# A decoder layer on one core: exponential before clip in the cross attention, key sums on TensorE

## What is computed

```
q, k, v = (x @ Wq.T + bq), (ctx @ Wk.T + bk), (ctx @ Wv.T + bv)     # per head
scores = einsum('bhsd,bhtd->bhst', q, k) / sqrt(32)
scores = clip(scores, -50, 50)
scores = where(attend, scores, -10000)
scores = clip(scores, -50, 50)
probs  = softmax(scores, axis=-1)
probs  = probs / (probs.sum(axis=-1, keepdims=True) + 1e-8)
ctx    = einsum('bhst,bhtd->bhsd', probs, v)
delta  = layernorm(rs * (ctx @ Wo.T + bo)) * gamma + beta
x      = layernorm(x + delta)
```

## Time and profile before

| | |
|---|---|
| median of three runs | 1547.76 us (1546.38 to 1550.83) |
| profiled execution | 1548.03 us |
| its span | 1546.1 us |
| mean granted clock of PE | 0.963 |
| PE, DVE, ACT, POOL busy in the span | 90%, 81%, 50%, 48% |
| DVE clip (line 1081), 64 instructions | 1213 ns each (median) |
| ACT exponential (line 1276), 64 instructions | 79.0 us, 1239 ns each |
| POOL sum of halves (line 1338), 32 instructions | 76.1 us, 2378 ns each |

### The profile page before, as it was taken

One profiled execution on the slowest core, in us unless ns is written; L12 is line 12 of the kernel. 1 busy time (PEld: TensorE's weight loads), 2 busy tenths in 40 slices (PEclk: granted clock), 3 DMA queues, 4 the chain that ended last, 5 costly groups with the idle time before them and its releaser, 6 DMA issues.

```text
span 1546.1 us, 25019 instructions
## 1 busy us (share of the span) xinstructions
PE 1395.2 (90%) x8338; PEld 1093.7 (71%) x8338; DVE 1257.5 (81%) x2029; ACT 766.7 (50%) x1710; POOL 744.2 (48%) x781
## 2 busy tenths in 40 slices
PE   5899999999999999999999999779999996359985
PEld 4788888888888888888888888667766674213332
DVE  6988888888888888888888888456899998759996
ACT  4444544444544445455455554444444444048885
POOL 4334334335235234334334333624766676547984
PEclk9999999999999999999999999989999998668998
DMA  5401101101011011012121110410000004004433
GB/s 206 163 2 42 64 6 41 50 19 41 27 42 41 27 42 28 22 49 68 42 69 55 34 61 15 143 42 15 15 15 14 14 1 170 0 20 91 90 87 95
DMA packets 73380, 79.91 MB, mean 52 GB/s; under 512 B 46007, under 2 KB 46519, under 8 KB 72893
## 3 DMA queue, kind: packets, MB, share of 16 engines
q1 hardware_dynamic: 73276, 78.73, 16.6%
HBM read 59.83 MB, written 8.40 MB: 44 GB/s over the span
## 4 chain that ended last, share of the span: by engine, by line
PE 40%; DVE 35%; issue 11%; POOL 11%; ACT 2%; DMA 1%; DVEq 1%; SPq 0%; POOLq 0%; ACTq 0%
PE psum L326 9%; PE psum L328 8%; PE psum L327 8%; DVE rope_b L513 6%; PE psum L367 3%; DVE p L522 3%; DVE total_e L526 3%; DVE xe L1081 2%; DVE acc L556 2%; DVE s L494 2%; DVE xinv L1088 2%; PE psum L388 2%; DVE rope_a L513 2%; PE psum L376 1%; PE psum L365 1%
## 5 line engine op out<-in xcount | busy, mean ns | idle before, releaser
L730 POOL TENSOR_TENSOR qk<-rope_a,rope_b 128x512 f32<-128x512 f32 x128 | 177.3, 1385 | 569.2 <-DVE rope_b L513 569.2
L326 PE MATMUL psum<-x_hi,w_hi 128*128 128x512 f32 x512 | 210.5, 411 | 11.2 <-POOL w_lo L724 11.2
L328 PE MATMUL psum<-x_hi,w_lo 128*128 128x512 f32 x512 | 201.2, 393 | 0.0
L327 PE MATMUL psum<-x_lo,w_hi 128*128 128x512 f32 x512 | 200.5, 392 | 0.0
L513 DVE SCALAR_TENSOR_TENSOR rope_b<-psum,qk_bias,sin 64x512 f32<-64x512 f32 x256 | 192.0, 750 | 3.7
L604 ACT ACTIVATE e<-s 128x384 f32<-128x384 f32 x128 | 66.4, 519 | 242.9 <-DVE s L494 242.9
L494 DVE SCALAR_TENSOR_TENSOR s<-psum,tri 128x384 f32<-128x384 f32 x128 | 70.7, 552 | 121.3 <-PE psum L367 121.3
L326 PE MATMUL psum<-w_hi,x_hi 128*128 128x256 f32 x512 | 147.4, 288 | 0.0
L327 PE MATMUL psum<-w_lo,x_hi 128*128 128x256 f32 x512 | 144.7, 283 | 0.0
L328 PE MATMUL psum<-w_hi,x_lo 128*128 128x256 f32 x512 | 144.6, 282 | 0.0
L1276 ACT ACTIVATE xe<-xe,mask_now 128x1024 f32<-128x1024 f32 x64 | 79.0, 1239 | 129.1 <-DVE xe L1081 129.1
(11 more groups left out here) (179 smaller groups left out, 3890.1 us busy)
## 6 DMA issues: line engine op xcount, KB each, us to landing
stage<-w_self_dram SPq DMA_DIRECT2D x64, 256.0 KB, 2.9
w_raw<-w_ffn_dram SPq DMA_DIRECT2D x32, 512.0 KB, 3.6
acc<-xT_dram SPq DMA_DIRECT2D x4, 1024.0 KB, 7.6
acc<-x_dram SPq DMA_DIRECT2D x1, 4096.0 KB, 15.1
w_signs<-w_sign SPq DMA_DIRECT2D x16, 256.0 KB, 2.1
c_raw<-ctxT_dram SPq DMA_DIRECT2D x8, 512.0 KB, 3.6
xstage<-w_cross_dram SPq DMA_DIRECT2D x16, 256.0 KB, 2.9
w<-w_signs SPq DMA_DIRECT2D x2, 2048.0 KB, 11.4
```

Source lines behind the costliest of these rows:

```text
L326: pe.matmul(ps, ah, bh, start=n == 0, stop=False)
L327: pe.matmul(ps, ah, bl, start=False, stop=False)
L328: last = pe.matmul(ps, al, bh, start=False, stop=n == len(pairs) - 1)
L730: nc.gpsimd.tensor_tensor(qk[:, k % 2, which, :], rope_a[:, which, :], rope_b[:, which, :], ALU.add).then_inc(qk_ready, 1)
```

## The change

Three things, all in `cross_attention`:

- `exps` reads the scores from the banks and writes `e`; it counts up `exped`, which also frees the banks for the next scores. It waits for the scores (`s_mm`) once per chunk.
- `clip` follows it, in place in SBUF, with exp(50) and exp(-50) as bounds, once per half, and waits for `exped` of its half. It counts up `e_ready`.
- `sum_e`, `e_sum` and its semaphore are gone. PE multiplies both halves of `e` with the ones, eight matmuls in place of four, and adds them in the bank.

```diff
@@ score
-                wait(pe, clipped, (b * CH + c) * HALVES)
+                wait(pe, exped, (b * CH + c) * HALVES)
@@ mix
-                pe.wait_ge(e_summed, b * CH + c + 1)
-                for h in range(HEADS_IN):
-                    last = pe.matmul(psA[h * H:(h + 1) * H, S:2 * S], ones[:], e_sum[:, h, :], start=True, stop=True,
-                                     tile_position=(0, h * H))
+                for kt in range(HALVES):
+                    for h in range(HEADS_IN):
+                        last = pe.matmul(psA[h * H:(h + 1) * H, S:2 * S], ones[:],
+                                         e[:, c % 2, h, kt * S:(kt + 1) * S], start=kt == 0, stop=kt == 1,
+                                         tile_position=(0, h * H))
@@ clip
-                dve.wait_ge(s_mm, b * CH + c + 1)
-
                 for kt in range(HALVES):
-                    nc.vector.tensor_scalar(e[:, c % 2, :, kt * S:(kt + 1) * S], scored[:, :, kt, :], LIMIT, -LIMIT,
-                                            ALU.min, ALU.max).then_inc(clipped, 1)
+                    dve.wait_ge(exped, (b * CH + c) * HALVES + (kt + 1))
+                    part = e[:, c % 2, :, kt * S:(kt + 1) * S]
+                    nc.vector.tensor_scalar(part, part, EXP_MOST, EXP_LEAST, ALU.min, ALU.max).then_inc(e_ready, 1)
@@ exps
-                act.wait_ge(clipped, (b * CH + c) * HALVES + (kt + 1))
-                part = e[:, c % 2, :, kt * S:(kt + 1) * S]
-                nc.scalar.activation(part, part, ACT.Exp, scale=mask_now[:, par, kt, 0:1],
-                                     bias=mask_now[:, par, kt, 1:2]).then_inc(e_ready, 1)
+                if kt == 0:
+                    act.wait_ge(s_mm, b * CH + c + 1)
+                nc.scalar.activation(e[:, c % 2, :, kt * S:(kt + 1) * S], scored[:, :, kt, :], ACT.Exp,
+                                     scale=mask_now[:, par, kt, 0:1], bias=mask_now[:, par, kt, 1:2]
+                                     ).then_inc(exped, 1)
@@ sum_e (POOL), and its call in emit
-            def sum_e(b, c):
-                pool.wait_ge(e_ready, (b * CH + c + 1) * HALVES)
-                wait(pool, av_mm, b * CH + c)
-                nc.gpsimd.tensor_tensor(e_sum[:], e[:, c % 2, :, 0:S], e[:, c % 2, :, S:2 * S], ALU.add
-                                        ).then_inc(e_summed, 1)
```

More of the change, by code:

```diff
@@ L1 @@
+import math
 from contextlib import ExitStack
@@ L789, in cross_attention @@
     LIMIT = 50.0
+    EXP_MOST, EXP_LEAST = math.exp(LIMIT), math.exp(-LIMIT)
     v_proj = env["shared_sems"]["v_proj"]
@@ L821, in cross_attention @@
         e = sb("xe", [P, 2, HEADS_IN, 2 * S])
-        e_sum = sb("e_sum", [P, HEADS_IN, S])
         o32 = sb("o32", [P, 2, S])
@@ L858, in cross_attention @@
         s_mm = sem("s_mm")
-        clipped = sem("clipped")
+        exped = sem("exped")
         e_ready = sem("xe_ready")
-        e_summed = sem("e_summed")
         av_mm = sem("av_mm")
@@ L1382, in emit @@
                             split_c(b + 2)
-                    if live(b):
-                        sum_e(b, i)
                     pb, pc = before(b, i)
```

## The result

The kernel with the change took 1564.38 us, the median of four runs (1563.13 to 1565.26); the kernel before, run beside it, took 1547.07. The ratio is 1.0108, with a 95% interval of 1.0087 to 1.0130: slower, by 17.3 us, where the prediction said slower by 13 to 14.

The account below looks back on a forecast made before the run. Cross attention was taken as bound by PE and DVE, both nearly always busy, and the waits between them. Five batches +12.3, batches 0 and 1 +6.2, last batch -5.6 gave +12.9 us: 1561 us, range 1533 to 1575.

Parts of the forecast that it names:

- The wait that is added: DVE's second clip waits for ACT's second exponential, itself behind work waiting for PE; the query projection starts 1.1 us later.
- The clip: DVE's clip of 1024 elements, in SBUF instead of PSUM: 0.7 us, from 1213 ns; bounds 0.54 and 1.21.
- Rival (c): The clip gets no faster in SBUF, so DVE is not relieved as claimed: 1572 us; chance 0.15.
- The exponential: ACT's exponential of 1024 elements out of PSUM: 1.24 us, as out of SBUF, starting with the scores.
- Part 0: PE's stretch from the first chunk's scores to the second's: 8.31 + 0.45 + a wait of 0.4 = 9.2 us.
- Part 1: PE's stretch from the second chunk's scores to the third's: 11.11 + 0.45 = 11.56 us.
- Part 2: PE's third chunk: 3.8 to x's transposes, 7.05 to the query projection, 1.6 for it: 12.45 us.
- the block of 0.6 us: GpSimd's operations hold up DVE's clip in Part 1 by half an operation, 0.6 us; bounds 0 and 1.3.
- Part 3: PE's stretch from the fourth chunk's scores to the next batch: 7.34 + 0.45 = 7.8 us.
- The lower clock: PE's clock drops around the stop before the query projection: three batches at 1.2 us each, 3.6 together.
- part 2 twice, 2.2: In batches 0 and 1, the longer Part 2 counted twice: 2.2 us of their +6.2.
- (a): DVE is the bound and is relieved; PE becomes the bound at 36.4 us a batch: 1531 us; chance 0.17.

Follow-up runs that it names:

- Experiment 1: The changed kernel with ACT issuing both exponentials of a chunk before the piece that waits for PE: 1534.57 us, ratio 0.9913.
- experiment 6: The changed kernel with DVE doing the division of the chunk before ahead of the two clips: 1531.47 us, ratio 0.9898.
- experiment 5: The changed kernel without its clips, the matmuls waiting for the exponential itself: 1516.78 us, ratio 0.9795.
- experiment 4: The kernel before with the sums moved from GpSimd to TensorE and nothing else: 1526.20 us, ratio 0.9863.
- experiment 9: The changed kernel with DVE's clips behind the division everywhere and, in Part 2, behind take_x as well: 1522.84 us, ratio 0.9830.
- experiment 2: The kernel before with ACT issuing both exponentials of a chunk together, ahead of the piece that waits for PE: 1541.17 us, ratio 0.9953.

## Why the prediction was right, and where by luck

The forecast was 1561 us, the runs gave 1564.38, and the mechanism it rested on is the one that the experiments show. By its steps:

- **The wait that is added**: right. DVE's idle time before the second clip of batch 5, released by ACT, was 2.32, 3.87, 1.98 and 0.81 us in parts 0 to 3; I had asked for some 3 us in parts 0 and 1. Experiment 1 shortens it by ACT's order, experiment 6 leaves the late exponential and puts the division ahead of it on DVE, and both turn the loss into a gain. PE's stop before the query projection was 3.09 us for the 3.4 that I gave as a sign; by my own walk it should have been 7.05 less the 3.9 for which PE is busy, 3.15.
- **The clip**: 0.69 us where nothing disturbs it, for a forecast of 0.7. Rival (c), in which it is no faster in SBUF, fell with that.
- **The exponential**: 1.206 us out of PSUM for a forecast of 1.24.
- **Part 0**: 9.53 us in batch 5 for 9.2, since PE waited 0.71 for the division and not 0.4. The wait for the key copy is gone, as forecast.
- **Part 1**: 11.55 for 11.56.
- **Part 2**: the sum was 3.8 + 7.05 + 1.6. The middle term measured 6.97. The first was 3.15 in batches 2 to 5, so the block of 0.6 us that I put on part 1's clip was not there (0.69 us at 1243.99), and the wait for x with it. That was luck of position: in each of these four batches the clip began in a pause of 0.26 us between two of GpSimd's operations (last section). Only batch 6 had one, 1.74 for 0.69, with PE waiting 0.64 for x and part 2 at 12.64. Zero was the lower bound that I had named. A block that I did not foresee fell on the first clip of part 3 in batches 0 to 5 (1.85 to 2.07 us, beside GpSimd's subtraction). It cost nothing, as DVE waited for the second exponential after it. The third term was 1.63 in batch 6, at the full clock.
- **Part 3**: 7.44 in batch 6, at the full clock, for 7.8. I had taken the 7.34 before batch 5; batches 1 and 6 of the kernel before show 7.00, which with the sums' 0.45 gives 7.45.
- **The lower clock**: I counted three such batches, and it was four. Batches 2 to 5 have a mean granted clock of 0.92 to 0.96, batch 6 has 1.00. In batch 5 the query projection took 2.86 us (1256.58 to 1259.44) where batch 6 needed 1.63. Added up over the query projections and the parts 3 of batches 2 to 5, against batch 6, it is 6.9 us for the 3.6 of the forecast.

So five batches came to +12.9 for a forecast of +12.3, but parts 2 and 3 were forecast some 1.0 us a batch too dear, part 0 0.3 too cheap, and the clock 3.3 in all too cheap: the terms were off in both directions and cancel. That the sum is so near is luck; the chain of part 2, 6.97 us for 7.05, is not. Batches 0 and 1 came to +7.9 for +6.2 (1098.91 and 1090.99 are the starts of batch 2). The step that was mis-sized there is "part 2 twice, 2.2": in batch 1 alone part 2 rose by 2.6 us (12.27 for 9.65), as its query projection also ran at the lower clock, and part 3 by 1.3. The last batch came to -5.8 for -5.6 (from the start of its scores to the last division, 1308.08 to 1343.93, against 1287.26 to 1328.92 in the trace of before):

```profile
1343.93 0.42 DVE L1092 SCALAR_TENSOR_TENSOR o<-psum,xinv 128x256 f32<-128x256 f32 x1
```

Of the rivals, (a) is what the change would have been with another order: its "PE's parts without waits, 36.4" is 35.93 us in experiment 5, and experiments 4, 6 and 9 come within 1.3 us of that. What I did not see was the worth of removing GpSimd's sums. I priced it at 1.9 us a batch of blocks on DVE and at the addition and blocks of the last batch, and saw nothing of the root behind the sums in GpSimd's queue; alone it was worth 21.8 us in all, with 2.5 us in each of batches 2 to 6, although PE has 1.8 us more to do there. The forecast did not suffer, because it was walked part by part and not summed from savings: in that walk, the swap's own chain was the later one.

## What to carry to other kernels

Swapping two steps on different engines swaps who waits for whom, and the price is not in the two steps but in what is queued behind the one that now waits. Before such a swap, read on both engines what stands ahead of the producer and behind the consumer: here moving the division and x_lo ahead of the clips on DVE turned +17 us into -26. And when an operation is taken out of a queue, look at what stood behind it before valuing it by its own length.

## What the runs showed of the hardware that I had not expected

**GpSimd's operations and DVE's clip in SBUF exclude each other, and either can be the one that waits.** The clip took 0.69 us alone, 2.07 us beside the subtraction of 2.40 us, and 1.74 beside an addition of 1.30. After, DVE in part 3 of batch 4 and POOL beside it:

```profile
1220.90 2.07 DVE L1082 TENSOR_SCALAR xe<-xe 128x1024 f32<-128x1024 f32 x1 [1.60 <-ACT xe L1276]
```

```profile
1220.03 2.40 POOL L1329 TENSOR_TENSOR c_lo<-c_raw,c_hi 128x1024 fp32r<-128x1024 f32 x1
```

The clip ends 0.54 us after the subtraction. The other way round, while the clip of 1243.99 ran in its 0.69 us, GpSimd's addition at 1244.14 took 1.70 us, where 1.30 is usual:

```profile
1244.14 1.70 POOL L1359 TENSOR_TENSOR acc<-acc,y 128x512 f32 x1 [0.26 <-POOL y L1356]
```

The rule of the Trainium skill (SBUF — State Buffer, "SBUF: two separate sides"), that of a DVE operation that uses both ports and a GpSimd operation the one that starts first keeps the other out for the whole instruction, agrees with these rows. It agrees as well where I had put the block at half an operation. POOL around the clip of 1243.99, and POOL and DVE at the same place of batch 6:

```profile
1242.59 1.29 POOL L1356 TENSOR_TENSOR y<-y,beta 128x512 f32<-128x512 f32 x1
```

```profile
1285.43 1.30 POOL L1359 TENSOR_TENSOR acc<-acc,y 128x512 f32<-128x512 f32 x1
```

```profile
1285.53 1.74 DVE L1082 TENSOR_SCALAR xe<-xe 128x1024 f32<-128x1024 f32 x1 [4.01 <-ACT xe L1276]
```

In batches 2 to 5 the clip began in the pause of 0.26 us before GpSimd's last addition (1243.88 to 1244.14 in batch 5) and was not held up; in batch 6 it began 0.10 us after that addition, and was. Not all of DVE's work is concerned: the statistics of line 1110, from SBUF, took 0.69 us beside GpSimd's operation of 1238.07, and the reciprocal, from PSUM, 1.75 beside that of 1244.14, the same as elsewhere.

**The clock after a stop.** In batches 2 to 6 PE stopped for 3.05 to 3.09 us before the query projection each time. From the table by stretches, around two of these stops:

```profile
1171.00:1176.00 5.00, 4.19 (x24) 3.81 (x28) 4.80 (x13) 1.22 (x4) 3.90 (x4) 0.50 0.02 5
...
1297.00:1302.00 5.00, 2.99 (x36) 2.42 (x40) 4.81 (x13) 1.66 (x4) 1.42 (x2) 1.00 0.00 0
```

The first is at the lower level, 1.2 GHz, throughout; the second stays at 2.4 GHz. PE had paused for 0.64 us before the second one's transposes, and for nothing before the first one's. Of five stops of one length, four were followed by the lower clock and one was not, so the length alone does not decide: in the kernel before, of five such stops of 2.07 to 2.11 us, those of batches 2 and 5 were followed by a stretch at 0.50 and three were not. What decides it these runs don't tell. In experiments 1, 4, 5, 6 and 9, in which no stop in the steady batches is longer than about 1 us, and in experiment 2, with stops of up to 1.64, the granted clock of that stretch is 1.00, so that the clock's loss went with the longer stops and was not a cost of its own.
